# DLRM tower on one core: a place for every gathered row, the middle groups written out, and the weight preparation moved

## The reference, cut to what matters

```python
e = jnp.stack([tbl_0[ids[:, 0]], ..., tbl_25[ids[:, 25]]], axis=1)   # 512 x 26 x 64
x = layer_norm(dense_t @ Wd.T, gd, bd)                    # 512 x 128
y = layer_norm(einsum('bnd,ed->bne', e, Ws), gs, bs)      # 512 x 26 x 128
y = layer_norm(einsum('bne,pn->bep', y, Wsi), gsi, bsi)   # 512 x 128 x 32
T = concatenate([x[:, None, :], swapaxes(y, 1, 2)], 1)    # 512 x 33 x 128
Z = einsum('bnd,bmd->bnm', T, T)
z = layer_norm(Z[:, TRIL_I, TRIL_J] @ Wl.T, gl, bl)       # 528 -> 512
z = z * (arange(512) < 384)
h = concatenate([z, dense_t], axis=1)
h = maximum(h @ W_top1 + b_top1, 0)                       # 768 -> 512
h = maximum(h @ W_top2 + b_top2, 0)                       # 512 -> 256
out = h @ W_top3                                          # 256 -> 1
```

## Time and profile before

| what | value |
|---|---|
| median of 3 runs | 245.53 us (245.27 to 246.01) |
| profiled execution, its own time | 243.04 us |
| its span | 241.2 us, 4708 instructions |
| TensorE (PE) busy | 173.7 us, 72%, 1983 passes |
| DVE busy | 121.1 us, 50% |
| ACT busy | 76.2 us, 32% |
| GpSimd (POOL) busy | 108.1 us, 45% |
| gathers, L285 | 104 of 1.00 us mean |
| mean granted TensorE clock | 0.83 of full speed |

### The profile page before, as it was taken

How to read it: one execution, slowest core, us unless ns; L and a number is a source line. 1 busy time by engine, 2 the same in 40 slices (tenths; PEclk the granted TensorE clock), 3 DMA queues, 4 the chain that set the end, 5 groups by cost and what they waited for, 6 DMA issues and landing times.

```text
span 241.2 us, 4708 instructions
## 1 busy us (share of the span) xinstructions
PE 173.7 (72%) x1983; PEld 131.6 (55%) x1983; DVE 121.1 (50%) x225; ACT 76.2 (32%) x158; POOL 108.1 (45%) x110
## 2 busy tenths in 40 slices
PE   0668825649981954689558728979929799867896
PEld 0318721235551724458528518846729686767695
DVE  6474400238958270546482920916863984773012
ACT  2021400026684420515321310414414165350224
POOL 3787777727775173456570660557450000330000
PEclk9985555757996796899875955997967999999999
DMA  6515453101111010010110010011010000000000
GB/s 190 178 24 125 111 155 97 45 5 26 28 22 29 3 30 16 14 22 16 20 26 8 16 24 6 11 24 22 16 27 0 0 0 1 0 3 5 0 3 0
DMA packets 5728, 8.14 MB, mean 34 GB/s; under 512 B 2357, under 2 KB 3279, under 8 KB 5712
## 3 DMA queue, kind: packets, MB, share of 16 engines
q0 software_dynamic: 3328, 3.41, 7.4%
q1 hardware_dynamic: 1664, 3.65, 5.0%
q10 hardware_dynamic: 720, 0.85, 1.2%
HBM read 7.91 MB, written 0.00 MB: 33 GB/s over the span
## 4 chain that ended last, share of the span: by engine, by line
PE 53%; issue 17%; another core or an unknown queue 13%; DVE 9%; ACT 5%; DMA 2%; ACTq 1%; DVEq 0%
PE ps_z L990 8%; PE ps_gq L947 6%; PE ps_y L968 5%; PE ps_ut L958 5%; PE ps_tail L1045 4%; PE ps_tail L1022 3%; PE ps_z L1002 3%; PE ps_tail L899 2%; DVE var L701 2%; DMA gs_sb<-in_gs_row_dram 2%; PE ps_y L1022 2%; PE ps_gq L941 2%; PE ps_tail L931 2%; PE ps_tail L1054 1%
## 5 line engine op out<-in xcount | busy, mean ns | idle before, releaser
L285 POOL DMA_INDIRECT G<-in_table_dram,idx x104 | 104.0, 1000 | 74.9 <-PE ps_ut L958 41.7
L990 PE MATMUL ps_z<-V 128*32 128x34 f32 x1024 | 21.1, 218 | 28.0 <-issue 26.3
L673 DVE TENSOR_TENSOR qg<-ps_gq,G 128x384 f32<-128x384 f32 (+1 forms) x16 | 9.4, 588 | 57.0 <-PE ps_gq L947 23.2
L990 PEld LDWEIGHTS ps_z<-V 128*32 128x32 f32 x1024 | 16.9, 128 | 35.3 <-issue 32.3
L968 PE MATMUL ps_y<-ut,wcg 64*128 64x512 f32 x64 | 21.6, 751 | 7.2 <-issue 7.0
L958 PE MATMUL ps_ut<-S,G 128*128 128x192 f32 (+4 forms) x128 | 25.1, 348 | 2.2 <-DVE G L686 1.5
L947 PE MATMUL ps_gq<-gram,gt 128*128 128x128 f32 x104 | 19.2, 335 | 8.9 <-ACT gt L367 7.7
L958 PEld LDWEIGHTS ps_ut<-S,G 128*128 128x128 f32 x128 | 23.5, 229 | 3.2 <-DVE G L686 2.1
L701 DVE TENSOR_REDUCE var<-sq 128x32 f32<-128x1024 f32 x16 | 19.4, 1213 | 8.5 <-ACT sq L381 7.9
L381 ACT ACTIVATE sq<-V 128x1024 f32<-128x1024 f32 x16 | 16.9, 1058 | 20.3 <-DVE V L696 20.3
L947 PEld LDWEIGHTS ps_gq<-gram,gt 128*128 128x128 f32 x104 | 16.4, 236 | 10.5 <-ACT gt L367 7.8
(11 more groups left out here) (138 smaller groups left out, 228.3 us busy)
## 6 DMA issues: line engine op xcount, KB each, us to landing
G<-in_table_dram,idx POOLq DMA_INDIRECT x104
w1z<-in_w_z_dram SPq DMA_DIRECT2D x1, 768.0 KB
wl<-in_wl_blocks_dram SPq DMA_DIRECT2D x1, 768.0 KB
dns<-in_dense_t_dram ACTq DMA_DIRECT2D x1, 512.0 KB
w1d<-in_w_d_dram SPq DMA_DIRECT2D x1, 512.0 KB
wl<-in_wl_blocks_dram SPq DMA_DIRECT2D x1, 512.0 KB
w2s<-in_w_dram SPq DMA_DIRECT2D x1, 512.0 KB
wrow<-in_wsi_rows_dram SPq DMA_DIRECT2D x1, 208.0 KB
```

The lines of the kernel that those rows point to most:

```text
L285: pool.indirect_dma_start(G[:, j, g, :], None, table, bass.IndirectOffsetOnAxis(ap=idx[:, k:k + 1], axis=0)).then_inc(gathered[c], 16)
L990: mm = pe.matmul(ps_z[32 * qb:32 * qb + 32, bb // 8, col:col + SLOTS], V[:, b, 0:NPROJ], V[:, b, :], start=True, stop=True)
```

## The change: own places for rows, no gather waits, groups written out, preparation moved

G gets a place for each group's rows (`[P, NG, TILES, 2, D]`), each chunk of each group its own semaphore, and GpSimd's waits go. The three `Fori` loops become Python loops, so their bodies stand twice in the program. The top bias becomes a row of 512 on one partition: `prepare_b1` has 3 products of 512 columns, b_top1 is loaded as a row by SyncE and added by DVE, and each `prepare_dense` adds it by a product of one row with a row of ones, all four blocks through the bank ps_tail. `prepare_b1`, `prepare_xsum` and the dense blocks stand later among the chunks, and so do ACT's `prepare_w1`, `prepare_means`, `prepare_gains` and DVE's `prepare_x`, `prepare_last_block` and `prepare_shift`.

```diff
         w2s = sb("w2s", [P, OC1, H2])
-        b1e = sb("b1e", [P, OC1])
+        b1e = sb("b1e", [1, H1])
         eps = sb("eps", [P, 1])
...
         h1_dense = sb("h1_dense", [P, OC1, B])
-        G = sb("G", [P, TILES, 2, D])
+        G = sb("G", [P, NG, TILES, 2, D])
         gt = sb("gt", [P, 4 * P])
...
         ld_wl = [sem("ld_wl_a"), sem("ld_wl_b")]
-        gathered = [sem(f"gathered{c}") for c in range(NC)]
+        gathered = [[sem(f"gathered{gp}_{c}") for c in range(NC)] for gp in range(NG)]
...
         yo_ps, yo_ready, stored = sem("yo_ps"), sem("yo_ready"), sem("stored")
-
-        def dense_bank(oc):
-
-            return ps_z[:, oc, :] if oc < 2 else ps_tail[:, :]
...
             sp.dma_start(w1z[:, :, :], w1_z).then_inc(ld_w1z, 16)
-
-            sp.wait_ge(gathered[0], 2 * len(batch(0)) * 16)
+            sp.dma_start(b1e[:, :], b1_row).then_inc(ld_w1z, 16)
+
+            sp.wait_ge(gathered[0][0], 2 * len(batch(0)) * 16)
             sp.dma_start(pmask[:, :], pair_mask).then_inc(ld_pm, 16)
...
             for h, (k, end) in enumerate(((0, 2), (2, KB))):
-                sp.wait_ge(gathered[1 + h], 2 * len(batch(1 + h)) * 16)
+                sp.wait_ge(gathered[0][1 + h], 2 * len(batch(1 + h)) * 16)
                 sp.dma_start(wl[:, k:end, :], wl_blocks[:, k:end, :]).then_inc(ld_wl[h], 16)
-            sp.wait_ge(gathered[3], 2 * len(batch(3)) * 16)
+            sp.wait_ge(gathered[0][3], 2 * len(batch(3)) * 16)
             sp.dma_start(w2s[:, :, :], w2).then_inc(ld_w2, 16)
...
                 for c in range(NC):
-                    if gp:
-
-                        pool.wait_ge(ut_ps, nth(gp - 1, c))
                     for j in batch(c):
...
                             pool.indirect_dma_start(
-                                G[:, j, g, :], None, table,
-                                bass.IndirectOffsetOnAxis(ap=idx[:, k:k + 1], axis=0)).then_inc(gathered[c], 16)
+                                G[:, gp, j, g, :], None, table,
+                                bass.IndirectOffsetOnAxis(ap=idx[:, k:k + 1], axis=0)).then_inc(gathered[gp][c], 16)
...
-                act.wait_ge(b1_ready, 1)
                 act.wait_ge(dense_ps, oc + 1)
-                act.activation(h1_dense[:, oc, :], dense_bank(oc), ACT.Identity, bias=b1e[:, oc:oc + 1]).then_inc(dense_ready, 1)
+                act.copy(h1_dense[:, oc, :], ps_tail[:, :]).then_inc(dense_ready, 1)
...
                 deviation2(gp - 1, 3)
-                prepare_gains((3, 4))
                 deviation1(gp, 1)
+                prepare_dense(2)
+                prepare_gains((0, 1))
...
                 z_evacuate(gp - 1, 1)
-                prepare_dense(2)
                 deviation1(gp, 2)
                 deviation2(gp, 0)
+                prepare_gains((2, 3, 4))
                 z_copy(gp - 1)
...
                 if first:
-                    prepare_means(1)
+                    prepare_dense(1)
                 square2(gp, 2)
...
                 deviation2(gp, 2)
+                deviation1(gp + 1, 0)
                 if first:
+                    prepare_means(1)
                     prepare_last_block()
-                deviation1(gp + 1, 0)
-                if not first:
+                else:
                     square2(gp, 3)
                     z_evacuate(gp, 0)
-                else:
-                    prepare_gains((0, 1, 2))
...
             deviation1(0, 0)
-            prepare_w1()
             gt_copy(0, 1)
...
             square2(0, 0)
+            prepare_w1()
             gt_copy(0, 2)
             ut_copy(0, 1)
-            prepare_xsum()
-            prepare_dense(0)
             deviation2(0, 0)
             deviation1(0, 2)
+            prepare_xsum()
             prepare_means(0)
-            prepare_dense(1)
+            prepare_dense(0)
             slots23(0, first=True)
             first_slots01(1)
-            with act.Fori(1, NG - 1) as gp:
+            for gp in range(1, NG - 1):
                 slots23(gp)
...
                 dve.tensor_tensor(qg[:, 0:n * P], ps_gq[:, 0:n * P],
-                                  G[:, js[0]:js[0] + n, :, :].rearrange("p j g d -> p (j g d)"),
+                                  G[:, gp, js[0]:js[0] + n, :, :].rearrange("p j g d -> p (j g d)"),
                                   ALU.mult).then_inc(q_used, 1)
...
                 dve.wait_ge(r1_ready, nth(gp, c))
-                rows = G[:, js[0]:js[0] + n // 2, :, :].rearrange("p j g d -> p (j g) d")
+                rows = G[:, gp, js[0]:js[0] + n // 2, :, :].rearrange("p j g d -> p (j g) d")
                 dve.tensor_tensor(rows, rows, r1[:, 0:n].unsqueeze(2).broadcast_to([P, n, D]), ALU.mult).then_inc(g_scaled, 1)
...
                 if first:
-                    prepare_shift()
+                    prepare_last_block()
                 variance1(gp + 1, 0)
                 normalise2(gp, 2)
+                y_evacuate(gp, 3)
+                scale_rows(gp + 1, 0)
+                variance2(gp, 3)
                 if first:
-                    scale_rows(gp + 1, 0)
-                y_evacuate(gp, 3)
-                if not first:
-                    scale_rows(gp + 1, 0)
-                variance2(gp, 3)
+                    prepare_shift()
...
             prepare_x_root(1)
+            variance1(0, 1)
+            scale_rows(0, 1)
             prepare_x()
             prepare_b1()
-            variance1(0, 1)
-            scale_rows(0, 1)
             x_slots(0, 0)
...
             variance1(0, 2)
+            scale_rows(0, 2)
             normalise2(0, 0)
-            scale_rows(0, 2)
             y_evacuate(0, 1)
-            prepare_last_block()
             slots23(0, first=True)
             first_slots01(1)
-            with dve.Fori(1, NG - 1) as gp:
+            for gp in range(1, NG - 1):
                 slots23(gp)
...
-                pe.wait_ge(ld_w1z, 16)
+                pe.wait_ge(ld_w1z, 32)
                 pe.wait_ge(ld_sm, 16)
-                for oc in range(OC1):
-                    for k in range(LLIVE):
-                        mm = pe.matmul(ps_tail[:, oc:oc + 1], w1z[:, k, oc * P:(oc + 1) * P],
-                                       sm[:, C_BL + k:C_BL + k + 1], start=(k == 0), stop=(k == LLIVE - 1))
+                for k in range(LLIVE):
+                    mm = pe.matmul(ps_tail[0:1, :], sm[:, C_BL + k:C_BL + k + 1], w1z[:, k, :],
+                                   start=(k == 0), stop=(k == LLIVE - 1))
                 mm.then_inc(b1_ps, 1)
...
-                    pe.wait_ge(x_sd_ready, 1)
-                if oc == 2:
+                    pe.wait_ge(xsum_ready, 1)
+                elif oc == 2:
                     pe.wait_ge(last_ready, 1)
-                if oc == 3:
-                    pe.wait_ge(dense_ready, 3)
+                else:
+                    pe.wait_ge(dense_ready, oc)
                 for k in range(2):
-                    mm = pe.matmul(dense_bank(oc), w1d[:, k, oc * P:(oc + 1) * P], dns[:, k, :],
-                                   start=(k == 0), stop=(k == 1))
-                mm.then_inc(dense_ps, 1)
+                    pe.matmul(ps_tail[:, :], w1d[:, k, oc * P:(oc + 1) * P], dns[:, k, :], start=(k == 0), stop=False)
+                pe.matmul(ps_tail[:, :], b1e[:, oc * P:(oc + 1) * P], zx[ROW_ONE:ROW_ONE + 1, :],
+                          start=False, stop=True).then_inc(dense_ps, 1)
...
                 pe.wait_ge(last_in_ready, 1)
-                pe.wait_ge(xsum_ready, 1)
+                pe.wait_ge(dense_ready, 2)
                 for k in range(KB):
...
                 js = batch(c)
-                pe.wait_ge(gathered[c], (gp + 1) * 2 * len(js) * 16)
+                pe.wait_ge(gathered[gp][c], 2 * len(js) * 16)
                 if not first:
...
                 for n, j in enumerate(js):
-                    mm = pe.transpose(ps_gq[:, n * P:(n + 1) * P], G[:, j, :, :].rearrange("p g d -> p (g d)"), eye[:, :])
+                    mm = pe.transpose(ps_gq[:, n * P:(n + 1) * P], G[:, gp, j, :, :].rearrange("p g d -> p (g d)"), eye[:, :])
                 mm.then_inc(gt_ps, 1)
...
                         begins = (P * j // NF) // CB != chunk or (P * j) % (CB * NF) == 0
-                        mm = pe.matmul(ps_ut[:, chunk % 2, col:col + n], G[:, j, :, :].rearrange("p g d -> p (g d)"),
+                        mm = pe.matmul(ps_ut[:, chunk % 2, col:col + n], G[:, gp, j, :, :].rearrange("p g d -> p (g d)"),
                                        S[:, j, :, :].rearrange("p s q -> p (s q)")[:, scol:scol + n],
...
-                    pe.wait_ge(dense_ready, 2)
+                    pe.wait_ge(x_sd_ready, 1)
                 else:
...
                 else:
-                    prepare_last_block()
+                    prepare_dense(1)
...
                 embed(gp, 3)
+                if first:
+                    prepare_last_block()
                 pair_products(gp, 0, first)
...
             gram_rows(0, 0)
-            prepare_b1()
```

(9 more changed lines are left out.)

10 lines of the change are left out of this document (4 added, 6 removed).

## The result

The changed kernel takes 294.03 us in the median (292.27 to 294.94, 4 runs), the kernel before 245.4 beside it. The ratio is 1.200 [1.189, 1.212]: 49 us more. The forecast was 262 us with a range to 272; the direction was right, the size was not.

What follows compares the result with a forecast made beforehand. TensorE was taken to be held beside gathers, GpSimd's waits giving its speed back. 139.2 + 119.7 - 0.7 - 0.5 = 257.7 us, 16.5 more than 241.2; added to the 245.53 median: 262 us, own range 257 to 272, 8-in-10 range 228 to 272.

Steps and rivals of the forecast that it cites:

- The gathers' end: On GpSimd: without waits, the other 70 gathers at 1.28 us each end their issue at 136.8 instead of 178.4.
- The feed: TensorE's progress beside gathers, 49.6 to 139.2 us: 3.1 passes per us, reaching pass 359 inside the second pair products.
- the low end's 144: TensorE at 139.2 us if fed 0.7 passes per us: pass 144, first pair products' start, span 266.5 us.
- The 1.5 us of aftermath: TensorE is let go 1.5 us after the last gather, so it is free at 139.2 us.
- The rest without gathers: TensorE's work after 139.2 us, stalls given back: 119.7 us from the first pair products, less 0.7 and 0.5.
- Written-out groups: Removing the loop of two rounds: taken as 0 us, with 0 and 6.1 us as ends.
- Preparation: Bias product reshaped and moved, dense blocks two passes more each: at most 0.7 us shows beside the feed.
- (c): The weight preparation part: bias product moved behind the first embedding; without the feed, gain 4 us and cost 3.7.
- Rival A: Gathers do not hold TensorE; slow pair products have another cause that goes with the waits: 184 us, chance 0.14.
- Rival B: TensorE's feed is better in one long gather stretch, 4.7 to 8 passes per us: 229 to 245 us, chance 0.18.
- Rival C: No change: progress beside and outside gathers is conserved, so pauses only move: 245.5 us, chance 0.05.

Runs made afterwards that it cites:

- the time with the waits: Changed kernel with GpSimd's twelve gather waits put back, all else kept: 246.17 us where the kernel before took 244.74, 195.77 where it took 187.48.
- the spaced gathers: Changed kernel with a chained 128x512 memset behind each gather of groups 1 to 3: 225.04 us (kernel before 244.74), 222.5 us (kernel before 187.48).
- the shorter pauses: Changed kernel with a chained memset behind each gather of groups 1 to 3: 197.72 us with 128x128, 207.22 with 128x256 (kernel before 188.24).
- plain transfers: Changed kernel, indirect gathers replaced by in-order transfers with chained memsets: every 1.79 us 231.95 us (kernel before 244.74), every 1.25 us 193.36 (kernel before 188.24).

## Why the prediction was wrong

**The gathers' end** was forecast at 136.8; the last was issued at 134.8 and took 0.95: right.

**The feed** is the step that failed. The forecast took 3.1 passes per us beside gathers, with 3.9 as the high end and 2.1 and 0.7 below. From 49.6 to 139.2 there were 29 passes in 89.6 us, 0.32 per us, and 35 when the kernel was run again. TensorE was at pass 92 instead of 359, not even at the low end's 144. The count was short from the start: the forecast put 81 passes before 49.6, as in the kernel before, and there were 63 (92 - 29). The 3.1 came from inside a torn pair product, where a few passes go every 0.7 us since nothing between them waits for another engine. The first groups' stretch is a chain of handovers: PE to ACT to PE to DVE, each with few passes. Beside unspaced gathers a wait for such a result lasts mostly 15 to 20 us, after a product of 2 passes as after one of 8. The unit should have been late results, not passes: the earlier trace rows had two (L958 to ACT, 8 to 9 us; L947 to DVE, 19.5 us), and I counted passes over the window around them.

**The 1.5 us of aftermath** was read from pair products too. The last gather's issue ended at 135.8, yet a result was late until 150.4 (9.31 us in the chain at 141.05). TensorE was let go near 149.9, some 11 us later than forecast.

**The rest without gathers** was well priced. From the first pair products to the end the sum has 127.3 us (266.5 - 139.2); it took 292.7 - 167.1 = 125.6. So the miss of 35.0 us against 257.7 divides into 10.7 (149.9 - 139.2), 17.2 for the 42 passes up to the first pair products (167.1 - 149.9), which I had placed beside gathers (it was at pass 98 and they start at 140), and 7.1 (125.6 - 118.5) for what lies between the first pair products and the middle of the second.

**Written-out groups** at 0: right, 1.002 [0.998, 1.006] in the free condition. It was not run alone in the held one; there loops, places and preparation together are 1.4 us, 9 at most by the interval. The Trainium skill's rule on branches ("Runtime: NRT & Kernel Launch", Instruction fetch mechanics) would, as the prediction read it, have shown here as a gain; no run shows one.

**Preparation** at 0 beside the hold: no difference that the runs can tell (1.4 us, at most 3.7% by the interval; none between the places). "Without the feed (c) would gain 4 us and cost 3.7" was wrong: it costs 8.6 us. The gain is 0.92 us, since TensorE then waits for rows. The product takes 4.57 us at a granted clock of 0.58, between the 2.7 and its double that the forecast named. The wait that it puts in front of DVE's y_evacuate (6.71 us) was not in the sum at all.

**Rival A** (gathers do not hold TensorE, 184 us) names a rule of the Trainium skill ("SBUF — State Buffer", opening): engine and DMA ports are apart and do not contend. In the free condition the traces agree, with pair products of 1.8 us beside gathers. In the held one TensorE is slower beside gathers, with 6.1 to 10.7 us, but no run shows that the ports are where it is held. It was the wrong rival for this result, but its number is about that of the kernel before in the other condition. The changed kernel itself was not run there.

**Rival B** (a better feed) fell with 0.32 passes per us. **Rival C** fell too: progress beside and outside gathers is not conserved, since spacing the same gathers took 21 us off the time with the waits.

## What to carry to other kernels

A wait that looks idle may be what lets another engine's results through; before taking it away, price what runs beside the work that it paused in handovers, not in instructions. A stall that no record explains should be measured again in another set of runs before it is built into a schedule: the spaced gathers gain 7% in one condition and, in the one run there is, cost 19% in the other. And work moved out of an engine's gap has to be priced with the waits that it puts ahead of other work on the engines that consume it.

## What was not expected of the hardware

- One kernel on one chip took 242.7 us in one set and 188.2 in another. In the held condition results of TensorE come up to 40 us late beside unspaced gathers, in the traces of the free one none does. What sets the condition no run tells.
- Torn pair products go on in steps some 0.73 us apart (142.05, 142.80, 143.53), or twice that (88.72 in the earlier trace rows follows 1.19 us of idle), of 1 to 5 passes. That is shorter than the 1.25 us from gather to gather, so a step isn't one per gather. Its cause stays open.
- In the held condition 0.30 us between gathers lets nearly nothing through, 0.8 us nearly all, once the first 13 us are over. Where between them the change lies is open: the shorter pauses ran in the free condition alone. So is whether the indirect form matters: plain transfers held nothing at 1.79 us, and ran at 1.25 us only where nothing is held.
- No version beats both kernels everywhere. In the held condition the spaced gathers do (225.04 us against 244.7 and 292.5); in the free one the kernel before and the one without waits but with the old preparation are level at 187 us, and no kernel with the right output was faster.
